# Moving part of the softmax sums of an attention kernel from TensorE to VectorE

## The chip, the cores and the metric

The kernel runs on one core of one Trainium2 chip. The metric is the device time of one execution in microseconds (us). TensorE does the matrix products, VectorE (DVE in the rows), ScalarE (ACT) and GpSimd (POOL) the elementwise work, SyncE (SP) issues DMAs. Tiles lie in SBUF, and TensorE writes its results to PSUM.

## The reference, cut to what matters

The model is a convolutional self-attention layer, a multi-head attention layer and a routed mixture of eight experts, on 4 images of 1024 tokens and 256 channels. The change touches the second of these alone:

```
qkv = (group_norm(x) @ w_qkv + b_qkv).reshape(B, N, H, 3, d)      # B=4, N=1024, H=8, d=32
scores = einsum('bnhd,bmhd->bhnm', q, k) / sqrt(d)
attn = softmax(scores, axis=-1)                                   # over m
vals = einsum('bhnm,bmhd->bnhd', attn, v)
```

There are 4 x 8 = 32 heads in all. Each needs the exponentials of a 1024 x 1024 matrix, their product with v, and their sum over m, by which the product is divided.

## The kernel before

**Stages.** Three stages follow one another: the convolutional attention (to about 353 us), the 32 heads (to about 836 us), and the projection, routing and experts. The change is in the heads.

**One head.** The scores are made transposed, in 8 blocks `m` of 128 keys by 1024 queries. For each block TensorE makes the scores (`scores`, L1016, two matmuls of 512 columns), ScalarE takes their exponential into `expd[:, m, :]` (L990, 128x1024 float32), and TensorE multiplies that with the values (`values`, L1030, four matmuls of 256 columns side by side). The sum over keys is also a matmul, with a tile of ones (`sums`, L1038, four of 256 columns). It isn't run on every block: GpSimd adds blocks 0 to 5 (`ADDED = 6`) into one tile `added` by five additions (L967), and TensorE sums `added` and blocks 6 and 7, which makes three `sums` a head.

**Maxima.** The softmax needs each query's maximum first. While one head runs, TensorE makes the untransposed scores of a later head (`maxima`, L211, two matmuls of 512 columns into the two halves of `ps_m`), and VectorE reduces each half (`block_max`, L217). `ps_m` holds one block only, so a matmul waits until VectorE has reduced what its half held before: the half of block i+1 waits for the same half of block i. After the last block of a later head VectorE takes the smallest (`least`, L227), TensorE turns the result (`max_turn`, L232), ScalarE and VectorE split it in two (L239, L244), and SyncE writes it into the later head's operands. TensorE waits for L244 before the first `values` of the head, because both use `ps_o`.

**Order.** Each engine runs an order written out by hand, with semaphores between them. TensorE's head is a loop over c = 0 to 3. Each pass runs `maxima(2c)`, `scores(2c)`, `scores(2c+1)`, `maxima(2c+1)`, and then a rest. At c = 0 the rest is `tail`, what is left of the head before (its blocks 6 and 7: two `values`, then two `sums`), and `max_turn`. At c = 1 it is the values of blocks 0 and 1 and `all_sums`, the sum over `added` of the head before. VectorE's head is a loop over i = 0 to 7 with `block_max` of block i in each, `least` behind i = 1, L244 behind i = 2, and the division of the head before behind i = 5. GpSimd's first addition of a head waits for the exponential of block 1. SyncE loads the operands of a head three ahead, when `pe_pv` says that the slot's last reader is done.

The first head has no `tail`; the last head's own sums are taken in `last_tail`. In the last two heads there are no `maxima` behind c = 0, and in the last one GpSimd adds nothing.

Of the kernel before, what the change touches and what calls it, by code (L numbers as in the profile page):

```python
# [27 lines left out]
ALU = mybir.AluOpType  # L28
# [6 lines left out]
NB = N // P  # L35
# [11 lines left out]
ADDED = 6  # L47
# [26 lines left out]
def flat(bank_pair):  # L74
    return bank_pair.rearrange("p a n -> p (a n)")
# [19 lines left out]
class Phase:  # L95
# [5 lines left out]
    def sb(self, name, shape, dt=F32):  # L101
        return self.ctx.enter_context(self.nc.sbuf_tensor(self.tag + name, shape, dt))
# [51 lines left out]
SLOTS = HG  # L154
# [708 lines left out]
def head_phase(nc, io, keep, sems, hd):  # L863


    with ExitStack() as ctx:
        ph = Phase(nc, ctx, "h_")
        sb, ps, sem = ph.sb, ph.ps, ph.sems
# [4 lines left out]
        expd = sb("expd", [P, NB, N])  # L873
# [12 lines left out]
        ones_in = sem("ones_in")  # L886
        pe_exp, pe_pv, pe_sum, pe_ot = sem("pe_exp", "pe_pv", "pe_sum", "pe_ot")
        a_exp, a_o, g_add = sem("a_exp", "a_o", "g_add")
        v_rc, v_norm = sem("v_rc", "v_norm")
        g_set, g_zero, pad_in = sem("g_set", "g_zero", "pad_in")  # L890
        consts = [(keep["w_pr"][:, :, :], io["w_pr"].rearrange("(t p) m -> p t m", p=P)),
                  (keep["w_rt"][:, :, :], io["w_rt"].rearrange("(t p) m -> p t m", p=P)),
# [5 lines left out]
        def stream(eng, head):  # L898

            head(0, 0, first=True)  # L900
            with eng.Fori(0, HEADS // SLOTS - 1) as t:
                for j in range(1, SLOTS + 1):
                    head(t, j)
            for j in range(1, SLOTS):
                head(HEADS // SLOTS - 1, j, left=SLOTS - 1 - j)

        with nc.Block() as block:

            @block.sync
            def _(sp):  # L910

                sp.dma_start(ones[:, :], io["allones"][:, 0:D]).then_inc(ones_in, 16)

                def head(t, j, first=False, left=SLOTS):
                    h = SLOTS * t + j
                    if left >= 1:
                        hd.max_rows(sp, t, j + 1)
                    if not first:
                        if left >= SLOTS - 1:

                            sp.wait_ge(pe_exp, NB * h)
                            sp.wait_ge(pe_pv, NB * h)
                            hd.load(sp, io, t, j + SLOTS - 1)
                        if j == 2:
                            sp.dma_start(keep["w2"][:, bass.ds(t, 1)].rearrange("p o k m -> p (o k m)"),
                                         io["w2"][bass.ds(t, 1)].rearrange("o p m -> (o p) m")).then_inc(sems["w_in"], 16)

                for j in range(EARLY, SLOTS):
                    hd.load(sp, io, 0, j)

                sp.wait_ge(hd.v_stored, 16 * B)
                stream(sp, head)

                for dst, src in consts:
                    sp.dma_start(dst, src).then_inc(sems["consts_in"], 16)
                for name, _ in TABLE_CONSTS:
                    sp.dma_start(keep[name][:, :], io[name]).then_inc(sems["table_in"], 16)
                sp.dma_start(keep["b1_t"][:, :, :], io["b1_t"]).then_inc(sems["bias_in"], 16)
                for b in range(2):
                    res_load(sp, io, keep, sems, b)  # L940
# [31 lines left out]
            @block.scalar  # L972
            def _(act):
                def outputs(t, j):
                    h = SLOTS * t + j
                    act.wait_ge(pe_sum, h + 2)

                    act.wait_ge(pe_ot, h + 1)
                    nc.scalar.activation(osum[:, :], ps_o[j % 2][:, :], ACT.Copy).then_inc(a_o, 1)

                def head(t, j, first=False, left=SLOTS):
                    h = SLOTS * t + j
                    for m in range(NB):
                        act.wait_ge(pe_exp, NB * h + m + 1)
                        if not first:

                            act.wait_ge(pe_pv, NB * (h - 1) + m + 1)
                            if m < ADDED:
                                act.wait_ge(g_add, (ADDED - 1) * (h - 1) + max(m, 1))
                        nc.scalar.activation(expd[:, m, :], flat(ps_e[m % 2]), ACT.Exp, scale=SCALE).then_inc(a_exp, 1)  # L990
                        if m == 1 and left >= 1:
                            hd.row_hi(act, ps_o[j % 2], t, j + 1)
                        if m == 3 and not first:
                            outputs(t, j - 1)
                        if m in (4, NB - 1) and not left:
                            values_in(m // 5)

                def values_in(i):

                    act.wait_ge(sems["pe_vt"], i + 1)  # L1000
                    nc.scalar.activation(vals_c[:, i, :], flat(ps_m), ACT.Copy).then_inc(sems["a_vt"], 1)

                stream(act, head)
                outputs(HEADS // SLOTS - 1, SLOTS - 1)

            @block.tensor
            def _(pe):
# [16 lines left out]
                        last = nc.tensor.transpose(ps_o[j % 2][:, q * P:(q + 1) * P], osum[:, q * P:(q + 1) * P], ident[:, :])  # L1024
                    last.then_inc(pe_ot, 1)

                def values(j, m):

                    for q in range(4):
                        mm = nc.tensor.matmul(ps_o[j % 2][q * D:(q + 1) * D, 0:QUARTER], vh[j % SLOTS][:, m, :],  # L1030
                                              expd[:, m, q * QUARTER:(q + 1) * QUARTER], start=(m == 0), stop=(m == NB - 1))
                    if m < ADDED:
                        mm.then_inc(pe_pv, 1)

                def sums(j, e, done, last=False):

                    for q in range(4):
                        mm = nc.tensor.matmul(ps_o[j % 2][q * D:(q + 1) * D, QUARTER:2 * QUARTER], ones[:, :],  # L1038
                                              e[:, q * QUARTER:(q + 1) * QUARTER], start=False, stop=last, skip_group_check=True)
                    mm.then_inc(done, 1)  # L1040

                def tail(j):
                    for m in range(ADDED, NB):
                        values(j, m)
                    for m in range(ADDED, NB):
                        sums(j, expd[:, m, :], pe_pv)

                def last_tail(j):

                    for m in range(ADDED, NB):  # L1050
                        values(j, m)
                    for m in range(ADDED, NB):
                        sums(j, expd[:, m, :], pe_sum if m == NB - 1 else pe_pv, last=(m == NB - 1))
# [11 lines left out]
                    by_token(nc, (ps_m, ps_e[0])[q], vals_c, w_pr, q).then_inc(sems["pe_pr"], 1)  # L1065

                def all_sums(t, j):
                    pe.wait_ge(g_add, (ADDED - 1) * (SLOTS * t + j + 1))
                    sums(j, added[j % 2], pe_sum, last=True)

# [59 lines left out]
            @block.vector  # L1130
            def _(dve):
                nc.vector.memset(rc8[0][:, :, :], 0.0).then_inc(v_norm, 1)

                def norm(t, j):

                    h = SLOTS * t + j
                    dve.wait_ge(pe_ot, h + 2)
                    dve.wait_ge(v_norm, h + 1)
                    turned = ps_o[j % 2][:, :].rearrange("p (k a q d) -> p k q a d", k=2, a=2, q=4)
                    nc.vector.reciprocal(rc8[j % 2][:, :, :], turned[:, 1, :, :, 0]).then_inc(v_rc, 1)  # L1140
                    dve.wait_ge(v_rc, h + 1)
                    nc.vector.tensor_tensor(vals_t[:, bass.ds(t, 1), :, j * D:(j + 1) * D].rearrange("p o (q a) d -> p (o q) a d", a=2),
                                            turned[:, 0, :, :, :],
                                            rc8[j % 2][:, :, :].rearrange("p q (a o) -> p q a o", o=1).to_broadcast([P, 4, 2, D]),
                                            ALU.mult).then_inc(v_norm, 1)

                def head(t, j, first=False, left=SLOTS):
                    h = SLOTS * t + j
                    for i in range(NB):
                        ahead = 1 if i < 2 else 2  # L1150
                        if left >= ahead:
                            hd.block_max(dve, ps_m, NB * h + LEAD + i, (j + ahead) % 2, (i + LEAD) % NB)
                        if i == 1 and left >= 1:
                            hd.least(dve, t, j + 1)
                        if i == 2 and left >= 1:
                            hd.row_lo(dve, ps_o[j % 2], t, j + 1)
                        if i == 5 and not first:
                            norm(t, j - 1)

                stream(dve, head)  # L1160
                norm(HEADS // SLOTS - 1, SLOTS - 1)

# [687 lines left out]
```

## Time and profile before

| | |
|---|---|
| time, median of 3 runs | 1238.78 us (1238.21 to 1240.36) |
| profiled execution, its own time | 1240.58 us |
| its span, first to last instruction | 1238.8 us |
| mean granted TensorE clock | 0.945 of full |
| TensorE busy in the span | 1124.2 us, 91% |
| VectorE busy | 676.7 us, 55% |
| GpSimd busy | 570.6 us, 46% |
| ScalarE busy | 434.1 us, 35% |

Times in rows are us from the start of the span, unless marked ns. `[x <-E]` behind a row of the timeline is idle time of its engine just ahead of it, and what ended it. TensorE's weight loads stand as an engine of their own, PEld. A float32 matmul of 256 columns leaves two records, so two blocks of `values` are 16 records. The end of a matmul is modelled, and neighbours overlap: starts are surer than ends.

### The profile page before, as it was taken

The numbers are of one execution on the slowest core, as the hardware profiler recorded it, in microseconds if no ns is written. First come the engines' busy times: TensorE is split into PE (matmuls) and PEld (weight loads), VectorE is DVE, ScalarE is ACT, GpSimd is POOL, SyncE is SP. The second block draws the span as 40 slices with busy tenths as digits, with TensorE's granted clock in tenths as the row PEclk, the third lists the DMA queues.
The fourth block names the chain that finished last, engine by engine and source line by source line (L and its number), as shares of the span: only waits on it lengthen the run. The fifth ranks groups of instructions, "written<-read, shape, count | busy, mean of one in ns | idle before, by whom it ended". The sixth has DMA issues, their size and how long they took to land. (4 is left out here: it accounts for less than half of the span.)

```text
span 1238.8 us, 23452 instructions
## 1 busy us (share of the span) xinstructions
PE 1124.2 (91%) x7604; PEld 822.3 (66%) x7605; DVE 676.7 (55%) x1491; ACT 434.1 (35%) x511; POOL 570.6 (46%) x565
## 2 busy tenths in 40 slices
PE   6899999896679999999999999998726999999995
PEld 3577878685455555555555555556516999999994
DVE  4264747556467777777777777715742333333331
ACT  1303232320225555555555555564420111111110
POOL 0003030303047777877787878840361444444443
PEclk8799999897689999999999999998857999999998
DMA  6204361323152232323232323134455565565551
GB/s 210 60 1 128 135 188 68 119 87 131 73 167 76 80 94 60 94 60 94 60 94 67 101 68 100 31 121 136 149 118 175 194 215 193 191 203 208 191 193 61
DMA packets 61608, 148.44 MB, mean 120 GB/s; under 512 B 11360, under 2 KB 31776, under 8 KB 59904
## 3 DMA queue, kind: packets, MB, share of 16 engines
q1 hardware_dynamic: 53184, 123.39, 31.1%
q0 software_dynamic: 7536, 22.96, 5.6%
q10 hardware_dynamic: 848, 1.58, 0.5%
q8 instruction: 23, 0.38, 0.1%
q14 instruction: 17, 0.14, 0.0%
HBM read 104.58 MB, written 39.87 MB: 117 GB/s over the span
## 5 line engine op out<-in xcount | busy, mean ns | idle before, releaser
L217 DVE TENSOR_REDUCE s_nmax<-ps_v 128x1 f32<-128x512 f32 x484 | 311.3, 685 | 114.2 <-PE ps_v L211 104.0
L967 POOL TENSOR_TENSOR h_added<-h_added,h_expd 128x1024 f32<-128x1024 f32 x124 | 295.5, 2383 | 37.6 <-ACT h_expd L990 29.7
L990 ACT ACTIVATE h_expd<-ps_v 128x1024 f32<-128x1024 f32 x128 | 131.1, 1025 | 155.5 <-PE ps_v L1016 150.0
L1713 PEld LDWEIGHTS ps_h<-xs_c,lnt 128*128 128x128 f32 x1248 | 147.0, 194 | 4.8 <-issue 2.9
L1713 PE MATMUL ps_h<-xs_c,lnt 128*128 128x128 f32 x1248 | 147.5, 277 | 2.3 <-DVE xs_c L1665 2.3
L1723 PE MATMUL ps_y<-w,vals_t 128*128 x624 | 141.2, 379 | 0.6 <-DVE ys L1678 0.6
L1030 PE MATMUL h_ps_o<-h_expd,s_vh 128*32 128x256 f32 x2048 | 137.8, 387 | 0.0
L424 POOL TENSOR_TENSOR a_res<-a_res,a_lnt 128x2048 f32<-128x2048 f32 x4 | 18.2, 4539 | 253.0 <-DVE a_lnt L123 253.0
L990 ACT ACTIVATE h_expd<-h_ps_e 128x1024 f32<-128x1024 f32 x128 | 130.3, 1018 | 0.0
L1754 ACT ACTIVATE vals_t<-ps_h 128x1024 f32<-128x1024 f32 x39 | 39.9, 1024 | 255.8 <-DVE ps_h L1658 255.8
L1723 PEld LDWEIGHTS ps_y<-w,vals_t 128*128 128x128 f32 x624 | 115.5, 190 | 15.1 <-issue 1.0
L594 PE MATMUL a_ps_v<-a_val,a_expd 128*128 128x257 f32 x512 | 120.2, 388 | 5.1 <-ACT a_expd L464 4.5
L1658 DVE TENSOR_TENSOR ps_h<-ps_h,b_t 128x1024 f32<-128x1024 f32 x39 | 48.1, 1232 | 130.3 <-PE ps_h L1713 130.3
L594 PEld LDWEIGHTS a_ps_v<-a_val,a_expd 128*128 128x128 f32 x512 | 98.2, 194 | 23.5 <-ACT a_expd L464 6.5
L1555 POOL TENSOR_TENSOR pause<-pause 128x1 f32<-128x1 f32 x156 | 30.6, 196 | 156.0 <-DVE ys L1678 131.5
L967 POOL TENSOR_TENSOR h_added<-h_expd 128x1024 f32<-128x1024 f32 x31 | 73.8, 2380 | 56.2 <-ACT h_expd L990 56.2
L1030 PEld LDWEIGHTS h_ps_o<-h_expd,s_vh 128*32 128x32 f32 x2048 | 53.7, 109 | 52.0 <-issue 22.5
L715 DVE TENSOR_REDUCE a_nmax<-a_ps_m 128x1 f32<-128x512 f32 x64 | 41.2, 685 | 62.7 <-PE a_ps_m L554 62.7
L211 PE MATMUL ps_v<-s_stk2m,s_stk2n 96*128 96x512 f32 x128 | 51.9, 453 | 3.2 <-issue 3.1
L1176 POOL DMA_INDIRECT xs_scr<-lnt,pos x32 | 31.4, 982 | 50.6 <-DVE pos L1417 41.4
L211 PE MATMUL ps_v<-s_stk3m,s_stk3n 96*128 96x512 f32 x128 | 51.4, 446 | 0.0
L211 PE MATMUL ps_v<-s_stk1m,s_stk1n 96*128 96x512 f32 x116 | 46.6, 446 | 0.0
(222 smaller groups left out, 1592.2 us busy)
## 6 DMA issues: line engine op xcount, KB each, us to landing
lnt<-in_w SPq DMA_DIRECT2D x38, 1024.0 KB, 4.9
qk_scr<-a_head_hi SPq DMA_DIRECT2D x16, 512.0 KB, 2.6
qk_scr<-a_head_lo SPq DMA_DIRECT2D x16, 512.0 KB, 3.6
w<-in_w SPq DMA_DIRECT2D x8, 1024.0 KB, 5.9
xs<-xs_scr SPq DMA_DIRECT2D x39, 128.5 KB, 2.1
a_x_t<-in_x_t POOLq DMA_DIRECT2D x4, 1024.0 KB, 9.2
r_scr<-a_res POOLq DMA_DIRECT2D x4, 1024.0 KB, 6.1
v_scr<-res SPq DMA_DIRECT2D x4, 1024.0 KB, 3.8
```

Of the source, the lines that this page charges most:

```text
L211: self.nc.tensor.matmul(ps_m[:, half, :], n_st[0:STACK, nb * P:(nb + 1) * P], m_st[0:STACK, half * HALF:(half + 1) * HALF], start=True, st ...
L217: self.nc.vector.tensor_reduce(self.nmax[k][:, nb, half:half + 1], ps_m[:, half, :], AX.X, ALU.max, negate=True).then_inc(self.v_max, 1)
L594: last = nc.tensor.matmul(ps_v[:, j % 2, 0:C + 1], expd[:, m, j * P:(j + 1) * P], val[b % 2][:, m, :], start=(m == 0), stop=(m == NB - 1))
L715: nc.vector.tensor_reduce(nmax[b % 2][:, nb, half:half + 1], ps_m[:, half, :], AX.X, ALU.max, negate=True).then_inc(v_max, 1)
L967: nc.gpsimd.tensor_tensor(total[:, :], (expd[:, 0, :] if m == 1 else total[:, :]), expd[:, m, :], ALU.add).then_inc(g_add, 1)
L990: nc.scalar.activation(expd[:, m, :], flat(ps_e[m % 2]), ACT.Exp, scale=SCALE).then_inc(a_exp, 1)
L1030: mm = nc.tensor.matmul(ps_o[j % 2][q * D:(q + 1) * D, 0:QUARTER], vh[j % SLOTS][:, m, :], expd[:, m, q * QUARTER:(q + 1) * QUARTER], star ...
L1176: pool.indirect_dma_start(io["xs_scr"][:, :], bass.IndirectOffsetOnAxis(ap=keep["pos"][:, i:i + 1], axis=0), keep["lnt"][:, i, :], None).t ...
L1658: nc.vector.tensor_tensor(blocks, blocks, b1_t[:, bass.ds(e, 1), :].rearrange("p o (k n) -> p (o k) n", n=1).to_broadcast([P, KC, P]), ALU ...
L1713: last = nc.tensor.matmul(ps_h[k][:, c // 4, c % 4 * P:(c % 4 + 1) * P], w1_now[k][:, t, c * P:(c + 1) * P], xs_c[:, t, :], start=(t == 0) ...
L1723: last = nc.tensor.matmul(ps_y[:, 0:C], hid_t[k][:, c, :], w2[:, bass.ds(e, 1), c, :].rearrange("p o n -> p (o n)"), start=(c == 0), stop= ...
L1754: nc.scalar.activation(hid_t[k].rearrange("p k n -> p (k n)"), flat(ps_h[k]), ACT.Gelu).then_inc(a_gelu, 1)
```

## The change

VectorE adds block 7 of the exponentials of a finished head onto its block 6, in place, behind `least` (i = 1) of the next head. It waits until TensorE has read block 7 for `values`. `tail` keeps its two `values` and loses its two `sums`. One `sums` over the pair comes at c = 1, ahead of the sum over `added`. ScalarE's exponential of block 7 waits for VectorE's addition. `pe_pv` still rises by 8 a head, but two of its steps stand at other places.

```diff
@@ ScalarE, head @@
-                            act.wait_ge(pe_pv, NB * (h - 1) + m + 1)
+                            act.wait_ge(pe_pv, NB * (h - 1) + m + (1 if m < ADDED else NB - m))
+                            if m == NB - 1:
+                                act.wait_ge(v_pair, h)
@@ TensorE @@
-                def values(j, m):
+                def values(j, m, paired=False):
...
-                    if m < ADDED:
+                    if m < ADDED or (m == NB - 1 and paired):
                         mm.then_inc(pe_pv, 1)
...
                 def tail(j):
                     for m in range(ADDED, NB):
-                        values(j, m)
-                    for m in range(ADDED, NB):
-                        sums(j, expd[:, m, :], pe_pv)
+                        values(j, m, paired=True)
...
                 def all_sums(t, j):
+
+                    pe.wait_ge(v_pair, SLOTS * t + j + 1)
+                    sums(j, expd[:, ADDED, :], pe_pv)
                     pe.wait_ge(g_add, (ADDED - 1) * (SLOTS * t + j + 1))
                     sums(j, added[j % 2], pe_sum, last=True)
@@ VectorE, head @@
                         if i == 1 and left >= 1:
                             hd.least(dve, t, j + 1)
+                        if i == 1 and not first:
+
+                            dve.wait_ge(pe_pv, NB * (h - 1) + NB - 1)
+                            nc.vector.tensor_tensor(expd[:, ADDED, :], expd[:, ADDED, :], expd[:, ADDED + 1, :], ALU.add).then_inc(v_pair, 1)
```

## Rows read from the trace of the kernel before

**Rows 1.** Windows of 60 us (four heads): busy and records per engine, clock, DMA.

```profile
623.00:683.00 60.00, 59.98 (x508) 34.40 (x500) 44.47 (x81) 34.51 (x40) 47.69 (x21) 1.00 0.27 79
```

**Rows 2.** Timeline of TensorE, passes c = 0 and c = 1 of one head.

```profile
643.91 1.07 PE L1030 MATMUL h_ps_o<-h_expd,s_vh 128*32 128x256 f32 x16
644.79 1.05 PE L1038 MATMUL h_ps_o<-h_expd,h_ones 128*32 128x256 f32 x16
...
645.80 0.70 PE L211 MATMUL ps_v<-s_stk1m,s_stk1n 96*128 96x512 f32 x2
...
646.81 0.62 PE L1016 MATMUL h_ps_e<-s_stk3n,s_stk3m 98*128 98x512 f32 x2
647.27 0.89 PE L211 MATMUL ps_v<-s_stk1m,s_stk1n 96*128 96x512 f32 x2
648.09 1.07 PE L1030 MATMUL h_ps_o<-h_expd,s_vh 128*32 128x256 f32 x16
648.97 0.61 PE L1038 MATMUL h_ps_o<-h_added,h_ones 128*32 128x256 f32 x8
649.52 0.73 PE L211 MATMUL ps_v<-s_stk1m,s_stk1n 96*128 96x512 f32 x2
```

**Rows 3.** Timeline of TensorE's weight loads, same head, end of c = 1.

```profile
647.65 0.19 PEld L211 LDWEIGHTS ps_v<-s_stk1m,s_stk1n 96*128 96x128 f32 x1 [0.41 <-DVE s_nmax L217]
648.08 0.59 PEld L1030 LDWEIGHTS h_ps_o<-h_expd,s_vh 128*32 128x32 f32 x16 [0.25 <-DVE s_mrow_lo L244]
```

**Rows 4.** Timeline of VectorE, same head.

```profile
642.13 2.67 DVE L217 TENSOR_REDUCE s_nmax<-ps_v 128x1 f32<-128x512 f32 x4 [0.63 <-PE ps_v L211]
644.84 0.17 DVE L227 TENSOR_REDUCE s_nmaxes<-s_nmax 128x8 f32<-128x16 f32 x1
646.31 1.29 DVE L217 TENSOR_REDUCE s_nmax<-ps_v 128x1 f32<-128x512 f32 x2 [1.30 <-PE ps_v L211]
647.52 0.27 DVE L244 TENSOR_TENSOR s_mrow_lo<-h_ps_o,s_mrow_hi 8x128 fp32r<-8x128 f32 x1
```

**Rows 5.** Timeline of GpSimd, same head and start of the next.

```profile
644.93 2.38 POOL L967 TENSOR_TENSOR h_added<-h_expd 128x1024 f32<-128x1024 f32 x1 [1.85 <-ACT h_expd L990]
648.28 9.76 POOL L967 TENSOR_TENSOR h_added<-h_added,h_expd 128x1024 f32<-128x1024 f32 x4 [0.97 <-ACT h_expd L990]
659.92 2.38 POOL L967 TENSOR_TENSOR h_added<-h_expd 128x1024 f32<-128x1024 f32 x1 [1.89 <-ACT h_expd L990]
```

**Rows 6.** Line 801: ns min/median/max, first and last start.

```profile
L801 DVE TENSOR_TENSOR a_h_lo<-a_lnt,a_h_hi x8: 1206/1218/1226, 132.4 to 316.9; 128x1024 fp32r<-128x1024 f32 x8
```

**Rows 7.** Line 771, and timelines of VectorE and GpSimd at its last execution.

```profile
L771 DVE TENSOR_TENSOR a_gdev<-a_mvc,a_mg x4: 160/160/345, 120.3 to 305.0; 128x2 f32<-128x2 f32 x4
...
305.04 0.34 DVE L771 TENSOR_TENSOR a_gdev<-a_mvc,a_mg 128x2 f32<-128x2 f32 x1
...
300.86 4.51 POOL L426 TENSOR_TENSOR a_res<-a_res,a_b_pr 128x2048 f32<-128x2048 f32 x1
```

**Rows 8.** Timelines of VectorE and GpSimd, c = 0 and 1 of the second-last head.

```profile
811.17 0.28 DVE L244 TENSOR_TENSOR s_mrow_lo<-h_ps_o,s_mrow_hi 8x128 fp32r<-8x128 f32 x1 [1.35 <-ACT s_mrow_hi L239]
...
809.63 2.38 POOL L967 TENSOR_TENSOR h_added<-h_expd 128x1024 f32<-128x1024 f32 x1 [1.73 <-ACT h_expd L990]
```

**Rows 9.** SyncE's last load of a head, and that load's time to landing.

```profile
652.53 0.35 SPq L201 DMA_DIRECT2D s_vh<-v_scr  x1
...
s_vh<-v_scr SPq DMA_DIRECT2D x24, 128.0 KB, 2.6
```

**Rows 10.** Windows of the first stage, columns as in the first group.

```profile
54.70:58.00 3.30, 3.30 (x8) 2.66 (x9) 0.00 (x0) 0.00 (x0) 0.00 (x0) 0.50 0.21 84
...
88.10:89.80 1.70, 0.00 (x0) 0.00 (x0) 1.60 (x6) 0.00 (x0) 0.00 (x0) 1.00 0.00 0
89.90:93.00 3.10, 3.10 (x8) 1.02 (x9) 2.75 (x19) 0.27 (x1) 0.00 (x0) 1.00 0.01 3
18.90:21.50 2.60, 0.00 (x0) 0.01 (x1) 0.00 (x0) 2.05 (x3) 0.00 (x0) 1.00 0.97 241
24.00:30.00 6.00, 5.40 (x8) 2.30 (x8) 4.86 (x8) 0.00 (x0) 0.00 (x0) 0.50 0.00 0
```

More of the change, by code:

```diff
@@ L888, in head_phase @@
         a_exp, a_o, g_add = sem("a_exp", "a_o", "g_add")
-        v_rc, v_norm = sem("v_rc", "v_norm")
+        v_rc, v_norm, v_pair = sem("v_rc", "v_norm", "v_pair")
         g_set, g_zero, pad_in = sem("g_set", "g_zero", "pad_in")
```

## The prediction, made before the change was run

> **What bounds the kernel now.** I read the windows first, for the stage that the change touches. TensorE is busy all of 60 us over four heads at full clock, GpSimd 48 us, VectorE 44 us [rows 1]. By that alone, matmuls taken from TensorE would be time gained. The timelines of one head tell more. A head takes 659.92 - 644.93 = 14.99 us [rows 5]. In it TensorE is not free of VectorE: the second matmul of `maxima` of an odd block waits until VectorE has reduced the same half of the even block (0.41 us on the weight loads at 647.65), and the first `values` behind it waits for L244 [rows 3]. So c = 1 is paced by a loop: `maxima(2)` starts at 645.80 [rows 2], VectorE reduces its halves from 646.31 to 647.60 [rows 4], the last matmul of `maxima(3)` goes at 647.65 [rows 3], `values` at 648.09 [rows 2]. TensorE's busy time covers this, because the waits are shorter than a matmul's modelled length. VectorE has a hole of 1.30 us ahead of 646.31 [rows 4], which lies there because TensorE is running the two `sums` of the tail.
>
> **Part 1, two sums leave the tail.** Two blocks of `values` take 644.79 - 643.91 = 0.88 us, 0.44 a block, and `sums` has the same shape [rows 2]. The tail loses 0.88 us, and `max_turn` and `maxima(2)` come as much earlier, but no sooner than `least` ends (644.84 + 0.17 = 645.01, [rows 4]): at about 645.1 in place of 645.80, a lead of 0.7 us. It is worth something only if VectorE can reduce `maxima(2)` sooner too.
>
> **Part 2, one sum comes at c = 1.** It stands behind `values(1)`, where TensorE waits for nobody: +0.44 us a head, in full.
>
> **Part 3, VectorE's addition.** Its wait for block 7's `values` ends with them, at about 643.91 + 1.07 = 644.98 [rows 2], as `least` does at 645.01: the wait costs nothing, and the addition can start at about 645.02. It reads two tiles of 1024 in SBUF. The trace has that shape on VectorE with GpSimd idle: 1.22 us [rows 6]. This is the lower bound. Then it would end at 646.24, and the reductions of `maxima(2)` start (0.08 us ahead of that end, as neighbours overlap) at 646.16, against 646.31: the hole is filled, TensorE's lead of 0.7 shrinks to 0.15.
>
> But GpSimd's first addition starts at 644.93 [rows 5], some 0.09 us ahead, and runs 2.38 us. Does it slow the other? No addition on VectorE with two tiles in SBUF runs beside it in this stage. The nearest row is tiny: L771, two SBUF inputs of 2 elements, takes 160 ns three times and 345 ns once, and that once it started 0.33 us before a GpSimd addition ended (300.86 + 4.51 = 305.37) and ended with it, 0.02 us behind [rows 7]. I read it as held until the other was done. One case, but the place of its end is hard to get by chance.
>
> The Trainium skill says the same on the page "SBUF — State Buffer", section "Who interferes with whom": a VectorE instruction with two SBUF inputs and a GpSimd instruction that reads SBUF share a read interface, the one that starts first has it for its whole length, and the other blocks. It speaks against this change; by it the sum would be the one below, and without it that of the first rival.
>
> Taken so, the addition ends at 644.93 + 2.38 + 0.02 + (1.22 - 0.16) = 648.39, the upper bound. The reductions start at 648.31 in place of 646.31: 2.00 us later. What is queued behind it on VectorE is all of the loop: `maxima(3)`, L244 and the first `values` go 2.00 us later. The pair's sum follows: 2.00 + 0.44 = 2.44 us a head. The other passes have no cover to give this back: each starts its own loop with its own `maxima`.
>
> **Part 4, the other waits.** ScalarE's new wait for block 7 lies at c = 3, far behind the addition: nothing. GpSimd's second addition would start at 648.28 [rows 5], about when VectorE lets go; it has 1.89 us idle ahead of each head [rows 5] and a head that is longer by 2.4: nothing. SyncE's loads wait for `pe_pv` of `values(0)` now, not of the tail. In the head shown they end at about 652.53 + 0.35 + 2.6 = 655.5 [rows 9] and are needed at 645.80 + 14.99 = 660.8 [rows 2, 5]. 5.3 us are spare, and load and need move together: nothing.
>
> **The sum.** The addition runs in 31 heads. In 29 of them `maxima` runs at c = 1: 29 x 2.44 = 70.8 us. In the second-last, L244 comes at 811.17, and the blocked addition would end at 809.63 + 2.38 + 0.02 + 1.06 = 813.09 [rows 8]: 1.9 + 0.44 = 2.3 us. In the last GpSimd adds nothing: -0.44. Together +72.7 us. On the profiled execution's 1240.58 us that is 1313.3. That execution lies 1.8 us above the median of the runs; on the median, 1238.78 + 72.7 = 1311.5 us. I predict **1312 us**.
>
> **Rivals.**
> *VectorE goes first, or nothing blocks.* The lead of 0.09 us is short, and an instruction's start needn't be when it takes what it shares. Then GpSimd waits 1.2 us, which its 1.89 us hold. Per head: reductions 0.15 earlier, one sum more: +0.29, or +0.44 if the 0.15 is lost to the hand-over. Over 30 heads, less 0.44: +8 to +13, 1247 to 1252 us. For it speaks the short lead; against it that exponential and `least` follow from the same matmuls, so the order should hold in every head.
>
> *They share instead of blocking.* VectorE's addition would run at GpSimd's pace, 2.38 us, to 647.40: reductions 1.01 later, 1.45 us a head, 29 x 1.45 = 42, some 1281 us. A mixture of blocked and unblocked heads lands here too. L771's end speaks against the first.
>
> *The clock falls.* With the addition blocked, TensorE has nothing from the end of `scores(3)` (646.81 + 0.62 - 0.7 = 646.7) to the reduction's end at 649.0: 2.3 us. After an idle stretch of 1.7 us the granted clock stayed at 1.00 (2.4 GHz), and 2.5 us behind one of 2.6 us it stood at 0.50 (1.2 GHz) [rows 10]. 2.3 lies between. A short stretch at 0.50 is 3.3 us [rows 10] and costs half of it, 1.65 us. In a third of the heads that adds 16 us (1328), in all of them 48 (1360).
>
> *Faster.* Were VectorE's part free, TensorE would do one sum less in 31 heads: 31 x 0.44 = 13.6, 1225 us. For that the reductions of `maxima(2)` must start 0.44 us or more ahead of 646.31, so the addition would have to end before 645.95: in under 0.93 us, where the shape has never taken under 1.206 [rows 6]. This decides against it.
>
> **Chances.** Blocked, clock held: 0.52 (its own range 1303 to 1320). VectorE first: 0.21. Sharing or a mixture: 0.10. Blocked with the clock falling: 0.10. Within 0.2%, by gains that I don't see: 0.04. Faster: 0.03. The range 1247 to 1330 takes the blocked case, most of "VectorE first", the mixtures and the clock falling in up to a third of the heads, about 0.83. Some 0.2% (2.5 us) is what a measurement of this kernel can tell from no change. So: faster 0.03, within 0.04, slower 0.93.
>
> **What would show it.** Right: VectorE's new instruction stretched to 3.3 or 3.4 us, starting 0.1 us behind GpSimd's first addition and ending 1.1 us behind its end; L217 then at 2 us past its place, TensorE's hole ahead of `maxima(3)`, heads 17.4 us apart. "VectorE first": 1.22 us on VectorE, the first L967 stretched, heads 15.3 to 15.4 us apart. Wrong altogether: heads under 14.9 us apart, or an addition that takes 1.22 us while L967 keeps 2.38.

## The result, and the profile after

The changed kernel takes 1355.14 us (median of 4 runs, 1353.99 to 1357.89), the kernel before beside it 1239.57: a ratio of 1.0914, 95% interval 1.0886 to 1.0942. It is 116 us slower. The prediction said slower by 73, 1312 us, and its range ended at 1330. The sign and the main cause were right, the size was not.

The page's busy times and its line of granted clock (tenths of full, 40 slices), for the whole execution:

```profile
PE 1168.0 (86%) x7356; PEld 835.7 (62%) x7357; DVE 778.7 (58%) x1522; ACT 433.8 (32%) x511; POOL 583.3 (43%) x565
...
PEclk8899999886799888899889988889896899999998
```

The clock line is new in the slices of the heads. The windows show it finer: first the four-head window of [rows 1], then the pass c = 1 of one head in three pieces, ahead of the last columns PEclk, DMA share and GB/s:

```profile
623.00:683.00 60.00, 50.93 (x358) 28.35 (x357) 46.94 (x65) 28.06 (x33) 40.25 (x17) 0.91 0.22 64
643.40:645.50 2.10, 0.00 (x0) 0.00 (x0) 2.10 (x3) 1.52 (x2) 1.75 (x2) 1.00 0.00 0
645.70:649.10 3.40, 3.40 (x26) 1.40 (x30) 1.97 (x4) 0.00 (x0) 3.32 (x2) 0.50 0.01 2
649.20:660.00 10.80, 10.80 (x92) 6.09 (x80) 8.16 (x14) 6.28 (x7) 5.09 (x3) 1.00 0.32 85
```

TensorE does nothing from 643.4 to 645.5, then works 3.4 us at half clock, then at full. The timelines of the same head, VectorE (against [rows 4]), GpSimd (against [rows 5]) and TensorE (against [rows 2]):

```profile
641.34 0.17 DVE L227 TENSOR_REDUCE s_nmaxes<-s_nmax 128x8 f32<-128x16 f32 x1
641.55 3.35 DVE L1161 TENSOR_TENSOR h_expd<-h_expd 128x1024 f32<-128x1024 f32 x1
644.82 1.28 DVE L217 TENSOR_REDUCE s_nmax<-ps_v 128x1 f32<-128x512 f32 x2
```

```profile
641.43 2.38 POOL L967 TENSOR_TENSOR h_added<-h_expd 128x1024 f32<-128x1024 f32 x1 [2.80 <-ACT h_expd L992]
644.16 5.37 POOL L967 TENSOR_TENSOR h_added<-h_added,h_expd 128x1024 f32<-128x1024 f32 x2 [0.35 <-ACT h_expd L992]
...
660.22 2.38 POOL L967 TENSOR_TENSOR h_added<-h_expd 128x1024 f32<-128x1024 f32 x1 [3.07 <-ACT h_expd L992]
```

```profile
641.66 0.72 PE L211 MATMUL ps_v<-s_stk1m,s_stk1n 96*128 96x512 f32 x2
...
642.70 0.62 PE L1018 MATMUL h_ps_e<-s_stk3n,s_stk3m 98*128 98x512 f32 x2
645.56 1.39 PE L211 MATMUL ps_v<-s_stk1m,s_stk1n 96*128 96x512 f32 x2 [2.24 <-DVE s_nmax L217]
646.88 1.94 PE L1032 MATMUL h_ps_o<-h_expd,s_vh 128*32 128x256 f32 x16
648.59 0.87 PE L1040 MATMUL h_ps_o<-h_expd,h_ones 128*32 128x256 f32 x8
...
649.82 0.73 PE L211 MATMUL ps_v<-s_stk1m,s_stk1n 96*128 96x512 f32 x2
```

VectorE's addition starts 0.12 us behind GpSimd's first and takes 3.35 us; it ends at 644.90, which is 1.09 behind GpSimd's end (641.43 + 2.38 = 643.81). The reductions wait behind it, TensorE has its hole of 2.24 us, and the two blocks of `values` behind it take 648.59 - 646.88 = 1.71 us, where they took 0.88 [rows 2]. From `maxima(2)` to `maxima(4)` pass 8.16 us in place of 3.72 [rows 2]; a head takes 660.22 - 641.43 = 18.79 us in place of 14.99. The addition is held like this in 30 of the 31 heads; the median is 3.35. The shortest (1.66) is that of the last head, where GpSimd had only the tail of its last addition left. By lines (ns min/median/max), that addition and GpSimd's, of which the longest has grown to 3.17 us:

```profile
L1161 DVE TENSOR_TENSOR h_expd<-h_expd x31: 1662/3347/3402, 378.3 to 935.6; 128x1024 f32<-128x1024 f32 x31
...
L967 POOL TENSOR_TENSOR h_added<-h_added,h_expd x124: 2348/2380/3167, 365.4 to 933.8; 128x1024 f32<-128x1024 f32 x124
```

### The profile page after: what moved, and what is told of

The parts are those of the page before. It is cut to its first block and busy times, and to the rows that moved or that the text cites. A ratio compares the mean times of both kernels' runs of the same rounds, so it can differ in the third digit from the quotient of the medians.

```text
span 1352.1 us, 23015 instructions
## 1 busy us (share of the span) xinstructions
PE 1168.0 (86%) x7356; PEld 835.7 (62%) x7357; DVE 778.7 (58%) x1522; ACT 433.8 (32%) x511; POOL 583.3 (43%) x565
## 5 line engine op out<-in xcount | busy, mean ns | idle before, releaser
L967 POOL TENSOR_TENSOR h_added<-h_added,h_expd 128x1024 f32<-128x1024 f32 x124 | 309.0, 2492 | 104.8 <-ACT h_expd L992 99.3
L992 ACT ACTIVATE h_expd<-ps_v 128x1024 f32<-128x1024 f32 x128 | 131.0, 1024 | 164.1 <-PE ps_v L1018 163.1
L1032 PE MATMUL h_ps_o<-h_expd,s_vh 128*32 128x256 f32 x2048 | 152.3, 419 | 2.2 <-DVE s_mrow_lo L244 2.2
L1161 DVE TENSOR_TENSOR h_expd<-h_expd 128x1024 f32<-128x1024 f32 x31 | 102.1, 3295 | 5.3 <-PE h_ps_o L1032 4.8
L211 PE MATMUL ps_v<-s_stk2m,s_stk2n 96*128 96x512 f32 x128 | 54.9, 487 | 18.1 <-DVE s_nmax L217 15.5
L211 PE MATMUL ps_v<-s_stk3m,s_stk3n 96*128 96x512 f32 x128 | 55.5, 483 | 16.8 <-DVE s_nmax L217 16.7
L979 ACT ACTIVATE h_osum<-h_ps_o 128x512 f32<-128x512 f32 x32 | 19.1, 597 | 142.9 <-PE h_ps_o L1040 142.9
```

Of the source, the lines that this page charges most:

```text
L211: self.nc.tensor.matmul(ps_m[:, half, :], n_st[0:STACK, nb * P:(nb + 1) * P], m_st[0:STACK, half * HALF:(half + 1) * HALF], start=True, st ...
L967: nc.gpsimd.tensor_tensor(total[:, :], (expd[:, 0, :] if m == 1 else total[:, :]), expd[:, m, :], ALU.add).then_inc(g_add, 1)
L1161: nc.vector.tensor_tensor(expd[:, ADDED, :], expd[:, ADDED, :], expd[:, ADDED + 1, :], ALU.add).then_inc(v_pair, 1)
```

## The experiments

Two things were to be told apart. First, whether the addition is long because GpSimd's addition holds it (theory), because it is slow by itself, or because the two share. Second, whether the 116 us, less the 73 of the sum, are the clock, or some longer wait. Ratios are against the kernel before, run beside.

**GpSimd goes second.** GpSimd's first addition of a head waits for VectorE's:

```diff
                             if not first:
                                 pool.wait_ge(pe_sum, h)
+                                pool.wait_ge(v_pair, h)
```

> The changed kernel, but GpSimd's first addition of a head also waits until VectorE's addition is done; nothing else moves. Theory (VectorE's addition is held until GpSimd's running addition ends): with no GpSimd addition running it takes 1.22 us in place of 3.35, TensorE's hole ahead of maxima(3) is gone, the clock stays at 1.00, heads are 15.3 to 15.4 us apart, time 1247 to 1253 us (8 to 13 above the kernel before). Rival 1 (the addition is slow by itself, in place on a tile that TensorE has just read): it still takes 3.35 us, time 1355 or more. Rival 2 (the two share a port and slow each other in proportion): as the theory here.

1250.39 us, ratio 1.0078 (1.0061 to 1.0094). VectorE's line of the new instruction, and GpSimd's timeline:

```profile
L1162 DVE TENSOR_TENSOR h_expd<-h_expd x31: 1224/1226/1953, 379.1 to 832.9; 128x1024 f32<-128x1024 f32 x31
```

```profile
640.44 2.38 POOL L968 TENSOR_TENSOR h_added<-h_expd 128x1024 f32<-128x1024 f32 x1 [3.07 <-DVE h_expd L1162]
...
655.71 2.37 POOL L968 TENSOR_TENSOR h_added<-h_expd 128x1024 f32<-128x1024 f32 x1 [3.05 <-DVE h_expd L1162]
```

The addition takes 1.23 us, in the same place, on the same tiles: it is not slow by itself. (The longest, 1.95, is that of the last head, where GpSimd's additions of the head before still run.) Heads are 15.27 us apart. This is the time of the rival "VectorE goes first" (1247 to 1252), got by a wait. The wait costs GpSimd nothing that shows.

**One input.** VectorE reads one tile only, beside GpSimd's running addition:

```diff
-nc.vector.tensor_tensor(expd[:, ADDED, :], expd[:, ADDED, :], expd[:, ADDED + 1, :], ALU.add).then_inc(v_pair, 1)
+nc.vector.tensor_reduce(scratch[:, :], expd[:, ADDED, :], AX.X, ALU.add).then_inc(v_pair, 1)
```

> The changed kernel with VectorE's addition replaced by a reduction that reads block 6 alone (1024 columns, one SBUF input) into a scratch column; block 7 is left out of the sums. GpSimd starts as in the changed kernel and runs beside it. Theory (what is held is the second SBUF input): the reduction takes 1.2 us although GpSimd runs, heads 15.3 to 15.4 us apart, 1247 to 1253 us. Rival (any reading of SBUF by VectorE beside GpSimd is held): 3.3 us, time near 1355.

1251.61 us (one run). VectorE's reduction and GpSimd's first addition of the same head:

```profile
639.50 1.22 DVE L1161 TENSOR_REDUCE h_scratch<-h_expd 128x1 f32<-128x1024 f32 x1
```

```profile
639.39 2.38 POOL L967 TENSOR_TENSOR h_added<-h_expd 128x1024 f32<-128x1024 f32 x1 [2.56 <-ACT h_expd L992]
```

It starts 0.11 us behind GpSimd, as the addition did, and isn't held. So what is held has to do with the second input in SBUF, or with the output: the reduction also writes one column in place of 1024. The division of the same run speaks against the output. It has one input in SBUF and one in PSUM and writes 256 columns to SBUF; in the head shown it runs beside GpSimd's next additions, and it takes 0.42 us in every head:

```profile
L1145 DVE TENSOR_TENSOR vals_t<-h_ps_o,h_rc x32: 423/424/426, 387.9 to 851.3; 128x256 f32 x28, 128x256 f32<-128x256 f32 x4
```

That leaves the two inputs in SBUF. An output of 1024 columns with one input wasn't run.

**Half the addition.** Columns 0 to 511 alone:

```diff
-nc.vector.tensor_tensor(expd[:, ADDED, :], expd[:, ADDED, :], expd[:, ADDED + 1, :], ALU.add).then_inc(v_pair, 1)
+nc.vector.tensor_tensor(expd[:, ADDED, 0:HALF], expd[:, ADDED, 0:HALF], expd[:, ADDED + 1, 0:HALF], ALU.add).then_inc(v_pair, 1)
```

> The changed kernel with VectorE's addition over 512 of the 1024 columns; the other half of block 7 is left out of the sums. Theory (held until GpSimd's addition ends, then its own length): 3.35 - 512 / 0.96 ns = 3.35 - 0.53 = 2.82 us, heads 0.53 us shorter or more, where the shorter hole lets the clock stay up: 18.2 us with the clock falling, 16.9 with it held; 1340 or 1297 us. Rival (the two share and VectorE runs at a lower pace): half of 3.35, 1.7 us.

1326.71 us (one run), between the two times that the theory gave. The addition's line, TensorE's wait in one head, and three windows:

```profile
L1161 DVE TENSOR_TENSOR h_expd<-h_expd x31: 693/2817/2876, 373.7 to 909.5; 128x512 f32<-128x512 f32 x31
```

```profile
646.77 1.39 PE L211 MATMUL ps_v<-s_stk2m,s_stk2n 96*128 96x512 f32 x2 [1.69 <-DVE s_nmax L217]
```

```profile
443.00:503.00 60.00, 53.16 (x399) 29.12 (x399) 48.52 (x72) 30.74 (x37) 40.16 (x18) 0.97 0.23 64
623.00:683.00 60.00, 54.34 (x386) 29.91 (x382) 46.25 (x69) 28.33 (x34) 37.82 (x17) 0.91 0.18 48
...
646.60:653.00 6.40, 6.23 (x37) 3.11 (x38) 2.69 (x6) 0.67 (x2) 4.08 (x2) 0.50 0.36 107
```

2.82 us, as forecast to the hundredth: half the columns save 0.53 us, not half the time, so the two don't share. The hole is 1.69 us in the head shown, and the clock falls behind it in 17 of 29 heads (0.97 in one window of 60 us, 0.91 in another).

**The hole filled.** TensorE repeats `scores(3)` while it waits:

```diff
-                def scores(s, m):
+                def scores(s, m, times=1):
...
-                    for half in range(2):
+                    for half in (0, 1) * times:
...
-                        scores(j % SLOTS, i)
+                        scores(j % SLOTS, i, times=5 if i == 3 and not first and left >= 2 else 1)
```

> The changed kernel, with TensorE running the two matmuls of scores(3) five times over (the same result written again, 4 x 0.47 = 1.9 us) in the hole of 2.3 us where it waits for VectorE; all else as changed. Theory (the changed kernel's time is 2.44 us a head for the held addition and the added sum, and the rest, 1.3 us a head, is the clock that falls to 0.50 once a head because of the hole): granted clock 1.00 all through the heads, heads 17.4 us apart, about 1312 us in spite of the added work. Rival (the rest is a longer wait, not the clock): clock 1.00, time still about 1355. Rival (the fall comes from the lower number of matmuls, not from the hole): clock still falls, 1355 or more.

1317.13 us, ratio 1.0615 (1.0598 to 1.0633): 38 us less than the changed kernel, with more matmuls. TensorE's timeline of one head, and windows of four heads and of that pass:

```profile
641.68 0.72 PE L211 MATMUL ps_v<-s_stk2m,s_stk2n 96*128 96x512 f32 x2
...
642.71 2.43 PE L1018 MATMUL h_ps_e<-s_stk0n,s_stk0m 98*128 98x512 f32 x10
645.55 1.09 PE L211 MATMUL ps_v<-s_stk2m,s_stk2n 96*128 96x512 f32 x2 [0.41 <-DVE s_nmax L217]
646.57 1.07 PE L1032 MATMUL h_ps_o<-h_expd,s_vh 128*32 128x256 f32 x16
...
648.43 0.74 PE L211 MATMUL ps_v<-s_stk2m,s_stk2n 96*128 96x512 f32 x2
```

```profile
623.00:683.00 60.00, 57.71 (x441) 34.09 (x440) 50.18 (x72) 29.47 (x35) 43.35 (x18) 1.00 0.17 46
641.60:648.40 6.80, 6.30 (x49) 3.92 (x49) 5.88 (x6) 2.32 (x3) 6.36 (x3) 1.00 0.01 1
```

`maxima(3)` starts 645.55 - 641.68 = 3.87 us behind `maxima(2)`, in the changed kernel 3.90: VectorE holds it up as long. But the clock stays at 1.00, and from `maxima(2)` to `maxima(4)` pass 6.75 us and not 8.16, 1.41 us less. Whether it is the idle time or the smaller number of matmuls around it that lowers the clock, this run doesn't tell, because it changes both. The run is the prediction's main case, the held addition with the clock up, and 1317 lies in that case's own range (1303 to 1320).

**VectorE away without a hold.** Three reductions of one input in place of the addition:

```diff
+for k in range(3):
+    slow = nc.vector.tensor_reduce(scratch[:, k:k + 1], expd[:, ADDED, :], AX.X, ALU.add)
+slow.then_inc(v_pair, 1)
```

> The changed kernel with three reductions of 1024 columns, one SBUF input each, in place of VectorE's addition; block 7 is left out of the sums. Nothing is held by GpSimd and nothing holds GpSimd, but VectorE is away for 2 x 1.14 + 1.22 = 3.5 us, as long as in the changed kernel and 0.15 more. Theory (the time is lost by VectorE's absence alone, with the hole on TensorE and the clock's fall behind it): GpSimd's additions all at 2.38 us, clock at 0.50 once a head, heads 18.9 us apart, about 1361 us. Rival (what GpSimd loses, its second addition at up to 3.17 us, has a part in it): under 1350 us.

1365.38 us, ratio 1.1004 (1.0976 to 1.1032). VectorE's timeline, and the line of GpSimd's additions:

```profile
647.34 0.17 DVE L227 TENSOR_REDUCE s_nmaxes<-s_nmax 128x8 f32<-128x16 f32 x1
647.55 3.47 DVE L1162 TENSOR_REDUCE h_scratch<-h_expd 128x1 f32<-128x1024 f32 x3
...
666.25 0.17 DVE L227 TENSOR_REDUCE s_nmaxes<-s_nmax 128x8 f32<-128x16 f32 x1
```

```profile
L967 POOL TENSOR_TENSOR h_added<-h_added,h_expd x124: 2342/2368/2396, 366.2 to 944.4; 128x1024 f32<-128x1024 f32 x124
```

Heads are 18.91 us apart, as forecast, though GpSimd lost nothing (2.40 at most, where the changed kernel's longest was 3.17). The time goes by VectorE's absence. The total is 4 us above the forecast: in six of the heads the clock stays at 0.50 for 6.8 us in place of 3.4, and these take 20.0 us.

**No addition.** TensorE's part of the change alone:

```diff
-                            dve.wait_ge(pe_pv, NB * (h - 1) + NB - 1)
-                            nc.vector.tensor_tensor(expd[:, ADDED, :], expd[:, ADDED, :], expd[:, ADDED + 1, :], ALU.add).then_inc(v_pair, 1)
...
-                    pe.wait_ge(v_pair, SLOTS * t + j + 1)
```

> The changed kernel without VectorE's addition and the waits for it; block 7 is left out of the sums. What stays is TensorE's part: two sums fewer in the tail, one more at c = 1. By the steps of the prediction the reductions of maxima(2) start 0.70 us earlier and one sum of 0.44 us follows: -0.26 us a head, 31 heads, 8 us under the kernel before, 1231 us. Rival (TensorE is the bound, each sum counts in full): -0.44 us a head, 1226 us. Rival (the wait for VectorE's reductions takes the whole gain): 1240 us or above.

1237.60 us, ratio 0.9973 (0.9959 to 0.9987): 3.6 us less, not 8. Starts of `maxima` 0, 2, 4 and of the next head's 0:

```profile
640.68 0.73 PE L211 MATMUL ps_v<-s_stk0m,s_stk0n 96*128 96x512 f32 x2
...
644.26 0.73 PE L211 MATMUL ps_v<-s_stk1m,s_stk1n 96*128 96x512 f32 x2
...
648.42 0.73 PE L211 MATMUL ps_v<-s_stk1m,s_stk1n 96*128 96x512 f32 x2
...
655.48 0.73 PE L211 MATMUL ps_v<-s_stk1m,s_stk1n 96*128 96x512 f32 x2
```

In this head 648.42 - 644.26 = 4.16 us pass where 3.72 did [rows 2]: the one sum more, 0.44, in full. What c = 0 gives is less than the 0.70 of the step. VectorE's `least` in this head and in one two heads on, and TensorE's `maxima(2)` behind the second, tell why:

```profile
643.94 0.17 DVE L227 TENSOR_REDUCE s_nmaxes<-s_nmax 128x8 f32<-128x16 f32 x1
...
673.64 0.17 DVE L227 TENSOR_REDUCE s_nmaxes<-s_nmax 128x8 f32<-128x16 f32 x1
```

```profile
674.07 0.72 PE L211 MATMUL ps_v<-s_stk3m,s_stk3n 96*128 96x512 f32 x2
```

`maxima(2)` starts 644.26 - 644.11 = 0.15 us behind the end of `least` in the one and 674.07 - 673.81 = 0.26 in the other; `max_turn`, which waits for `least`, stands ahead of it. Over all heads the mean is 0.20, and 0.75 in the kernel before: the lead is 0.55, and with the sum of 0.44 that leaves 0.11 us a head, 3 us in all. Even with VectorE's addition free of charge the change would be worth 0.3%.

**Six additions on GpSimd.** The kernel before with block 6 added by GpSimd too; one sum is left in the tail:

```diff
-ADDED = 6
+ADDED = 7
+SPLIT = 6
...
                 def tail(j):
-                    for m in range(ADDED, NB):
+                    for m in range(SPLIT, NB):
                         values(j, m)
```

(Both loops of `last_tail` run over `range(SPLIT, NB)`, too.)

> The kernel before with GpSimd adding block 6 as well (six additions a head) and TensorE summing two tiles: the aim of the change by the engine that has 1.9 us spare a head. The one sum left in the tail stays there. Theory: six additions back to back take 6 x 2.45 = 14.7 us, so GpSimd becomes the bound at 14.7 us a head, 0.28 us less than before: 31 x 0.28 = 9 us, about 1231 us. Rival (GpSimd falls behind, because it can't take its additions back to back across heads): 15.5 us a head, 1255 us. Rival (TensorE's tail gives the whole 0.44): 1226 us.

1232.27 us, ratio 0.9937 (0.9919 to 0.9956): 0.6% less than the kernel before, little but clear of the noise. The profiled execution (1227.13 us) is the fastest of the six. Windows of four heads, the line of GpSimd's first additions, its waits for data, TensorE's waits for it, and `maxima(0)` of two heads on TensorE:

```profile
623.00:683.00 60.00, 59.97 (x492) 34.45 (x485) 45.24 (x82) 35.55 (x42) 58.35 (x26) 1.00 0.28 79
```

```profile
L968 POOL TENSOR_TENSOR h_added<-h_expd x31: 2365/2380/2401, 356.5 to 797.9; 128x1024 f32<-128x1024 f32 x31
...
  ACT h_expd L991: 1.6, 2
...
  PE h_ps_o L1039: 4.0, 2
```

```profile
645.55 0.73 PE L212 MATMUL ps_v<-s_stk1m,s_stk1n 96*128 96x512 f32 x2
...
660.10 0.73 PE L212 MATMUL ps_v<-s_stk2m,s_stk2n 96*128 96x512 f32 x2
```

TensorE's heads are 14.55 us apart, 0.44 less than before: the sum comes off in full, as in the second rival. But GpSimd doesn't keep that pace. Its first additions are (797.9 - 356.5) / 30 = 14.71 us apart, the 14.7 forecast; it falls behind a little in each head, and TensorE waits 4.0 us for it in the last two. GpSimd is busy 58.35 of 60 us and waits for data 1.6 us in the whole kernel: it has become the bound, and there is nothing left on it.

## Why the prediction was wrong in size

**The hold (part 3).** Right, to the digit. Forecast 3.3 to 3.4 us, starting 0.1 us behind GpSimd and ending 1.1 behind its end; measured 3.35, 0.12 and 1.09. The rivals for it fell: alone it takes 1.23, a reduction with one input isn't held, and half the columns take 2.82. The one execution of L771 [rows 7] had told it. The rule on the page "SBUF — State Buffer" of the Trainium skill (section "Who interferes with whom") agrees with all of these runs.

**The other terms of the sum.** "2.00 + 0.44 = 2.44 us a head": with the clock kept up, 29 such heads and the ends of the stage cost 1317.13 - 1241.21 = 76 us in the run with the hole filled, where the sum said 72.7. So this part was sized right. Inside it two smaller steps were off. The lead of 0.7 us that the tail was to give ("at about 645.1 in place of 645.80") is 641.66 against 641.34 + 0.17 in the profile after: `maxima(2)` starts 0.15 us behind `least` there and 0.20 in the mean, not 0.1. So the lead is some 0.55, and the run without an addition gained 3.6 us and not 8. This didn't enter the sum, where the lead is lost anyway. And "in the last GpSimd adds nothing" overlooked that GpSimd still had its last addition of the head before in hand: that addition on VectorE took 1.66 us.

**The clock: the step that failed.** The text had it as a rival, at 0.10, with its place ("2.3 us" without work ahead of `maxima(3)`) and its price ("in a third of the heads that adds 16 us (1328), in all of them 48 (1360)"), and the range took it "in up to a third of the heads". It fell once in each of the 29 heads in which `maxima` runs at c = 1. The place was right (2.24 us), and the price near it: 1.41 us in the head shown, 1355.14 - 1317.13 = 38 us in all, against 48. What failed is the step that weighed it: from one idle stretch of 1.7 us that the clock outlasted and one of 2.6 behind which it fell [rows 10], it took 2.3 as open, gave it little and put it into the sum at nothing. Two single events bound nothing that comes back 29 times. The trace of before had more to tell. The stretch at 0.50 from which the price came (54.70 to 58.00, [rows 10]) lies behind a hole of only 1.11 us, and the same matmuls of the next image, behind the same 1.11 us, ran at 1.00. The rows are from TensorE's timeline and the windows of the kernel before:

```profile
54.55 5.43 PE L594 MATMUL a_ps_v<-a_val,a_expd 128*128 128x257 f32 x16 [1.11 <-ACT a_expd L464]
...
106.58 3.75 PE L594 MATMUL a_ps_v<-a_val,a_expd 128*128 128x257 f32 x16 [1.11 <-ACT a_expd L464]
```

```profile
106.60:110.00 3.40, 3.40 (x17) 2.98 (x17) 0.00 (x0) 0.00 (x0) 1.65 (x2) 1.00 0.86 302
```

So the length of the last hole alone doesn't say whether the clock falls. The other runs agree: with half an addition holes of about 1.7 us were followed by a fall in some heads and not in others, and in the second-last head of the changed kernel a hole of 2.20 us wasn't followed by one:

```profile
926.60 1.07 PE L1032 MATMUL h_ps_o<-h_expd,s_vh 128*32 128x256 f32 x16 [2.20 <-DVE s_mrow_lo L244]
```

```profile
926.70:930.00 3.30, 3.30 (x40) 2.01 (x40) 0.00 (x0) 1.37 (x2) 3.16 (x2) 1.00 0.32 52
```

What does say it stays open. With the clock's price in all heads the same sum gives 1360, against 1355.

**The rest.** No other wait of part 4 shows up: GpSimd's second addition is held in turn (up to 3.17 us), and it costs nothing, as the three reductions show by costing as much without it. What stays open is why `maxima(2)` follows `least` by 0.15 us in half of the heads and by 0.26 in the others.

## What to carry to other kernels

Ahead of moving an addition of two SBUF tiles to VectorE, look at what GpSimd runs at that moment: what it costs is GpSimd's rest plus its own length, and everything queued behind it waits too. Where the sum of an edit leaves TensorE a new hole in a loop that ran at full clock, price the fall of the clock in every turn, as the likely case, until a row shows the loop doing without. And ask first whether the engine with the spare time can take the work itself: here GpSimd's 1.9 us a head took one more block and gave 0.6%, where VectorE's hole of 1.3 us only looked free.

## What the runs showed of the hardware that was not expected

Holes of about 2.1 to 2.24 us, one in each head of 18.8 us, were each followed by 3.4 us at 0.50 in 29 heads, and holes of about 1.7 us by a fall in 17 of 29, although one of 1.7 us in the first stage [rows 10] and one of 2.20 in the second-last head were not. Filling the hole with repeated matmuls kept the clock at 1.00 and made the kernel 38 us faster. The hold works both ways: when VectorE has begun, GpSimd's addition takes up to 3.17 us in place of 2.38.
